# Making the low parts of two hidden tiles in one VectorE instruction, in batches 1 to 15

## The reference, cut to what matters

```
h      = gelu(x @ fc1_w.T + fc1_b)            # 16 batches of 512 tokens, 512 -> 2048
shared = h @ fc2_w.T + fc2_b                  # 2048 -> 384
expert = h @ experts_w[indices].T + experts_b # 2048 -> 128, one expert per batch
x      = x + concat(shared, expert)
x      = x + masked_softmax_pooling(x)        # scores = v . tanh(W1 x + b1), prefix / suffix / all but own
```

## Time and profile before

| what | value |
|---|---|
| time, median of 3 runs | 1334.38 us (1334.28 to 1334.52) |
| span of the profiled execution, first to last instruction | 1332.5 us |
| median of the runs less that span | 1.9 us |
| TensorE busy | 1325.7 us, 99% |
| VectorE busy | 1252.0 us, 94% |
| ScalarE busy | 920.7 us, 69% |
| GpSimd busy | 7.4 us, 1% |

### The profile page before, as it was taken

The page is one execution under the profiler, slowest core; times in us unless marked ns, Lnnn a source line. Parts: engine busy times, 40 slices in busy tenths (PEclk is TensorE's granted clock), DMA queues, the critical chain, the costliest instruction groups (busy, mean ns, idle before and its releaser), DMA issues.

```text
span 1332.5 us, 22109 instructions
## 1 busy us (share of the span) xinstructions
PE 1325.7 (99%) x8685; PEld 850.9 (64%) x8685; DVE 1252.0 (94%) x2170; ACT 920.7 (69%) x1576; POOL 7.4 (1%) x12
## 2 busy tenths in 40 slices
PE   9999999999999999999999999999999999999998
PEld 4458476584856748567484765847658485674855
DVE  7998899999999999999999999999999999999998
ACT  5868858577694766948578585776847669485762
POOL 0000000000000000000000000000000000000002
PEclk9999999999999999999999999999999999999999
DMA  8410020110201102021020110202011020110106
GB/s 297 160 46 26 1 72 25 46 51 0 80 17 56 41 1 80 16 64 33 8 81 8 64 33 23 74 1 77 20 48 48 1 80 17 62 35 1 34 18 118
DMA packets 30520, 65.40 MB, mean 49 GB/s; under 512 B 6210, under 2 KB 7634, under 8 KB 27986
## 3 DMA queue, kind: packets, MB, share of 16 engines
q1 hardware_dynamic: 28690, 61.12, 14.0%
q0 software_dynamic: 1152, 2.09, 1.2%
q10 hardware_dynamic: 576, 0.79, 0.2%
HBM read 45.13 MB, written 18.87 MB: 48 GB/s over the span
## 4 chain that ended last, share of the span: by engine, by line
PE 99%; DMA 0%; DVE 0%; ACT 0%; ACTq 0%; DVEq 0%; issue 0%
PE ps L467 16%; PE ps L468 16%; PE ps L469 16%; PE ps L386 14%; PE ps L387 14%; PE ps L388 14%; PE ps L496 1%; PE ps L494 1%; PE ps L493 1%; PE ps L368 1%; PE ps L372 1%; PE ps L370 1%; PE ps L357 1%; PE ps L500 0%; DMA xr<-in_xT 0%; PE ps L581 0%
## 5 line engine op out<-in xcount | busy, mean ns | idle before, releaser
L469 PE MATMUL ps<-hl,w2h 128*128 128x512 f16 x768 | 291.1, 379 | 0.0
L467 PE MATMUL ps<-hh,w2l 128*128 128x512 f16 x768 | 291.1, 379 | 0.0
L468 PE MATMUL ps<-hh,w2h 128*128 128x512 f16 x768 | 291.1, 379 | 0.0
L387 PE MATMUL ps<-xl,w1h 128*128 128x256 f16 x960 | 261.7, 273 | 0.0
L388 PE MATMUL ps<-xh,w1l 128*128 128x256 f16 x960 | 261.7, 273 | 0.0
L386 PE MATMUL ps<-xh,w1h 128*128 128x256 f16 x960 | 261.7, 273 | 0.0
L742 ACT ACTIVATE g<-ps,b1s,ds 128x512 f32<-128x512 f32 x240 | 173.4, 773 | 88.3 <-PE ps L388 88.3
L386 PE MATMUL ps<-xh,ch 128*128 128x256 f16 x720 | 196.4, 273 | 0.0
L388 PE MATMUL ps<-xh,cl 128*128 128x256 f16 x720 | 196.3, 273 | 0.0
L387 PE MATMUL ps<-xl,ch 128*128 128x256 f16 x720 | 196.3, 273 | 0.0
L1218 DVE SCALAR_TENSOR_TENSOR hl<-g,ix,hh 128x512 f16<-128x512 f32 x243 | 176.8, 739 | 0.8
(11 more groups left out here) (259 smaller groups left out, 2384.8 us busy)
## 6 DMA issues: line engine op xcount, KB each, us to landing
xr<-in_xT SPq DMA_DIRECT2D x62, 256.0 KB, 3.1
er<-in_ew SPq DMA_DIRECT2D x15, 1024.0 KB, 5.6
out<-xr SPq DMA_DIRECT2D x60, 256.0 KB, 2.4
raw<-in_w SPq DMA_DIRECT2D x29, 256.0 KB, 5.9
er<-in_w SPq DMA_DIRECT2D x3, 1024.0 KB, 9.5
out<-sums POOLq DMA_DIRECT2D x8, 255.5 KB, 5.2
xr<-in_ew SPq DMA_DIRECT2D x1, 1024.0 KB, 6.2
out<-xn SPq DMA_DIRECT2D x3, 256.0 KB, 2.6
```

Source lines behind the costliest of these rows:

```text
L387: mm(to, wh, ml, start=False, stop=False, skip_group_check=True)
L467: mm(po(b, o), wl, hh[:, k, :], start=False, stop=False, skip_group_check=True)
L468: mm(po(b, o), wh, hh[:, k, :], start=False, stop=False, skip_group_check=True)
L469: m = mm(po(b, o), wh, hl[:, k, :], start=False, stop=k == NH - 1, skip_group_check=True)
```

## The change

The low parts of two neighbouring tiles are made by one instruction of 1024 columns. It waits for the high part of the second of the two tiles and adds 2 to `hl_done` at its end. Where steps of the pooling lay between the two `low`, those that lay between now come ahead of the merged instruction. Batch 0 keeps the single form.

```diff
@@ vector_program @@
+        def low_two(b, k):
+            e.wait_ge(hh_done, nth_tile(b, k + 1))
+            low_part(flat(hl[:, k:k + 2, :]), flat(g[:, k % GR:k % GR + 2, :]), scale_of(hc(b)),
+                     flat(hh[:, k:k + 2, :])).then_inc(hl_done, 2)
@@ the loop over the pairs, batches 1 to 15 @@
                 if c > 2:
-                    low(b, 2 * c - 6)
                     pool(one)
-                    low(b, 2 * c - 5)
+                    low_two(b, 2 * c - 6)
                 pool(two)
                 add_second(b, c - 1)
                 pool(three)
                 add_first(b, c)
...
-            low(b, 10)
             pool(2 if b == 1 else 1)
-            low(b, 11)
+            low_two(b, 10)
             pool(2 if b == 1 else 1)
             add_second(b, PAIRS - 1)
...
             expert_low(b, 0)
             expert_low(b, 1)
             pool(2)
-            low(b, 12)
-            low(b, 13)
+            low_two(b, 12)
             expert_low(b, 2)
             expert_low(b, 3)
-            low(b, 14)
-            low(b, 15)
+            low_two(b, 14)
```

## The result

The changed kernel takes 1339.61 us (1339.44 to 1339.87, 5 runs) against 1334.38 (1334.28 to 1334.55, 5 runs): 5.2 us more, a ratio of 1.004 with a 95% interval of 1.0029 to 1.0051. It is slower by 0.4%. The profiled execution has a span of 1337.6 us against 1332.5.

The account below looks back on a forecast made before the run. TensorE was taken as the bound, busy 84.00 us of 84.00 in mid-kernel. Stalls at tile 14, 14 x 0.35 = 4.9 us plus 0.27 in batch 2, add 5.2 to 1334.4: 1339.6 us, range 1337.2 to 1341.8.

Parts of the forecast that it names:

- TensorE bounds, and VectorE's time is worth nothing: Batches 3 to 14: TensorE never stands, so some 15.6 us less VectorE time gives the end nothing.
- The price of the merged instruction: VectorE, 1024 columns: 1.28 us, from 739 ns at 512 columns and 1010 ns at 768.
- The bounds of 1.22 and 1.41: Merged instruction's time: at least a plain addition's 1.22 us (total 1338.7), at most the two single ones' 1.41 (total 1341.6).
- The pairs of tiles 0 to 13 cost nothing: Merges ahead of the last pair: cost 0; the gelu needing tiles 10 and 11 has 3.5 us of room.
- a pooling step takes longer than a high part: Pairs of tiles 0 to 11, batches 2 to 15: a pooling step ahead covers the wait for the second high part.
- The start of the last pair doesn't move: Tiles 14 and 15, batch 7: still starts at 628.15; the 0.13 us saved ahead only lengthens VectorE's 0.61 us wait for ScalarE.
- The load 0.05 us after the end, the matmul with it, 0.35 us per batch: Tile 14, batch 7: merged instruction ends 629.43, load at 629.48, matmul due 629.14 goes 0.34 late, 0.35 with 0.01 on top.
- The 0.01 on top: TensorE at tile 14: small extra paid beyond the 0.34 us lateness of the matmul, making 0.35.
- The sum: Batches 1 and 3 to 15: 14 x 0.35 = 4.9 us; batch 2: 0.27 more; together 5.2 us.
- The weight load was forecast to wait 0.55 us: Sign in the changed profile: tile 14's load at L467 waits about 0.55 us for `hl` in every batch.
- the two rules of the Trainium skill: VectorE: larger operations can raise throughput if the engine is saturated; otherwise splitting may finish work sooner; tiles 14 and 15 show the second.

Follow-up runs that it names:

- the first experiment: Changed kernel with tiles 14 and 15 made by single instructions again, the other seven pairs still merged: 1334.55 us, ratio 1.0001.
- the kernel with the later wait: Changed kernel with TensorE's wait for the low part moved from ahead of a tile's first matmul to ahead of its third: 1334.41 us, ratio 1.0.

## Why the prediction was right

**TensorE bounds, and VectorE's time is worth nothing.** Right: with seven merges in and the eighth out, VectorE had 11.3 us less to do and the time was the same.

**The price of the merged instruction**, 1.28 us from the step between 512 and 768 columns: 1.28 in the timeline, 1272 ns in the mean over 120. The bounds of 1.22 and 1.41 were not needed. Of the saved VectorE time I expected 15.6 us, and 13.3 were found in its busy time; where the rest went is open, and nothing hangs on it.

**The pairs of tiles 0 to 13 cost nothing.** Right, by the first experiment. One reason that I gave doesn't hold as it stands: that a pooling step takes longer than a high part. A step can be as short as 0.60 us (the one at 629.48 in the earlier trace rows, with the next at 630.08), and the second of two high parts ends 0.61 us behind the first (1.33 less 0.72). It did no harm: VectorE's wait for the high parts of the hidden tiles is 10.5 us in both kernels.

**The start of the last pair doesn't move.** Right, and this was the step on which all hung: the wait for the expert quarters grew from 0.61 to 0.74 us in batch 7, by what had been saved since the wait before it.

**The load 0.05 us after the end, the matmul with it, 0.35 us per batch.** Right: 0.35 in batch 7, and a step of 81.57 us where I had written 81.55. The 0.01 on top belongs to the matmul behind the late one and comes in addition to the 0.35.

**The sum**, 14 x 0.35 and 0.27 for batch 2, 5.2 us. Measured 5.2. The mechanism is right; that the numbers agree to a tenth is in part luck. The steps add up to 14 x 0.365 and 0.25 for batch 2, nearly 5.4. But in the profiled execution the changed kernel came to batch 1 about 0.1 us sooner than the kernel before: L496 there is 0.25 us later (180.95 against 180.70), where the one stall up to there makes 0.36. And runs of one kernel lie up to 0.4 us apart. Batch 2 stands 0.35 as forecast, because VectorE's relief reaches it; the kernel with only the last merge shows the 0.6 us that it would have been otherwise.

The weight load was forecast to wait 0.55 us; it waits 0.68. The two aren't the same thing: I counted from when a load goes on its beat, the profile from the end of the load ahead, whose record is 0.10 us long where loads on their beat follow each other every 0.216 us.

Of the two rules of the Trainium skill that I set beside each other (Perfetto Trace Analysis, Optimizing Scalar/DVE Operations), the one on splitting instructions held here: single instructions for tiles 14 and 15 let TensorE go on sooner, 1334.55 us in the first experiment against 1339.61. The one on larger operations has a condition, a saturated engine, which VectorE at 94% didn't meet: it waited for ScalarE in front of the very work that mattered.

No version of these beats the kernel before. Three are as fast as it is with less VectorE work, and TensorE leaves them nothing to win in these batches.

## What to carry to other kernels

Merging two instructions delays the announcement of the first half by the time of the merged instruction less that of the first: here 1.28 less 0.74, 0.54 us. Before merging, look for who waits for the first half and how much room it has, in the one stretch where the room is smallest; the busy share of the merging engine, 94% here, says nothing on that. If the merge is wanted for another reason, put the consumer's wait directly ahead of the instruction that reads the data, or the merged instruction ahead of work that nobody is waiting for.

## What the runs showed of the hardware

In the kernel with the later wait, a weight load that goes 0.09 us ahead of its matmul's beat leaves the matmul on the beat (629.52 and 629.61 in batch 7), although the record of the load is 0.10 us long. In the changed kernel, a load that is later than the beat, due at 631.10, takes the matmul with it, at most 0.01 us behind (631.44 and 631.45). The usual lead is 0.21 us (629.18 and 629.39), and at 0.19 (628.95 and 629.14) and at 0.09 there was no price; what a lead between 0.09 and 0 costs no run here shows.
